# Cross-attention on one Trainium2 core: in each key tile TensorE does the side piece between the scores and the values

## The reference

```python
xq = ada_ln(x, cond, Wss_q, bss_q)            # x: (1, 4096, 512) f32
xkv = ada_ln(ctx, cond, Wss_kv, bss_kv)       # ctx: (1, 3202, 512) f32
q = (xq @ Wq + bq).reshape(B, Lq, 16, 32)
k, v = split((xkv @ Wkv + bkv).reshape(B, Lkv, 2, 16, 32))
scores = einsum('bqhd,bkhd->bhqk', q, k) / sqrt(32)
attn = softmax(scores, axis=-1)
out = einsum('bhqk,bkhd->bqhd', attn, v).reshape(B, Lq, 512)
return x + (out @ Wp + bp)
```

## Time and profile before

| | before |
|---|---|
| median of 3 runs | 2190.83 us |
| the profiled execution's own time | 2191.92 us |
| its span, first to last instruction | 2189.9 us |
| PE busy | 2162.7 us (99%) |
| DVE busy | 1895.0 us (87%) |
| ACT busy | 1820.4 us (83%) |
| granted TensorE clock, mean | 0.998 |

### The profile page before, as it was taken

How to read it: one execution, slowest core, us unless ns; L and a number is a source line. 1 busy time by engine, 2 the same in 40 slices (tenths; PEclk the granted TensorE clock), 3 DMA queues, 4 the chain that set the end, 5 groups by cost and what they waited for, 6 DMA issues and landing times.

```text
span 2189.9 us, 56660 instructions
## 1 busy us (share of the span) xinstructions
PE 2162.7 (99%) x25402; PEld 627.7 (29%) x25402; DVE 1895.0 (87%) x1098; ACT 1820.4 (83%) x1908; POOL 29.7 (1%) x29
## 2 busy tenths in 40 slices
PE   7999999999999999999999999999999999999998
PEld 3444322222222222222222222222222222222222
DVE  2321799989999899999999999989999999989998
ACT  1212899999999999999999899999999999999995
POOL 0000000000000000000000000000000000000000
PEclk9999999999999999999999999999999999999999
DMA  7322322223222422223222422223222322232211
GB/s 283 116 96 91 118 62 61 60 68 118 66 65 71 116 64 62 71 66 115 70 64 67 116 71 60 67 75 117 60 72 59 109 64 67 60 99 88 66 44 41
DMA packets 171445, 180.91 MB, mean 83 GB/s; under 512 B 14006, under 2 KB 117182, under 8 KB 171196
## 3 DMA queue, kind: packets, MB, share of 16 engines
q1 hardware_dynamic: 169612, 176.70, 27.0%
q10 hardware_dynamic: 1584, 0.53, 0.1%
HBM read 146.27 MB, written 30.92 MB: 81 GB/s over the span
## 4 chain that ended last, share of the span: by engine, by line
PE 97%; DMA 1%; DVE 1%; issue 0%; ACT 0%; SPq 0%; POOL 0%; DVEq 0%
PE bank L1024 39%; PE bank L1036 36%; PE bank L942 5%; PE bank L1112 4%; PE bank L1066 4%; PE bank L953 4%; PE bank L1048 1%; PE bank L1077 1%; PE bank L922 1%; DMA arena<-l_recip 1%; PE bank L1174 1%; PE bank L1088 1%; DMA arena<-in_ctx_dram 0%; DMA l_recip<-r_blk 0%; PE bank L1098 0%
## 5 line engine op out<-in xcount | busy, mean ns | idle before, releaser
L1282 ACT ACTIVATE arena<-bank,shift 128x1024 f32<-128x1024 f32 x1600 | 1692.2, 1113 | 162.2 <-PE bank L1024 154.5
L1567 DVE TENSOR_TENSOR arena<-arena 128x2048 f32<-128x2048 f32 x736 | 1669.7, 2289 | 110.4 <-ACT arena L1282 98.0
L1024 PE MATMUL bank<-qs,ks 32*64 32x512 f32 x12800 | 922.1, 613 | 1.1 <-ACT arena L1246 0.7
L1036 PE MATMUL bank<-arena,vg 128*32 128x512 f32 x6400 | 852.3, 605 | 1.3 <-ACT arena L1282 1.3
L1036 PEld LDWEIGHTS bank<-arena,vg 128*32 128x32 f32 x6400 | 125.9, 108 | 650.6 <-ACT arena L1282 649.0
L1024 PEld LDWEIGHTS bank<-qs,ks 32*64 32x64 f32 x12800 | 206.7, 129 | 346.8 <-ACT arena L1282 204.0
L1112 PE MATMUL bank<-wp,arena 128*32 128x168 f32 (+2 forms) x2464 | 153.6, 321 | 1.6 <-DVE arena L1496 1.6
L1066 PE MATMUL bank<-xt,wq 128*32 128x256 f32 x1792 | 137.7, 379 | 0.0
L1112 PEld LDWEIGHTS bank<-wp,arena 128*32 128x32 f32 x2464 | 80.0, 110 | 186.5 <-issue 170.0
L1433 DVE TENSOR_TENSOR arena<-bank,bv_b 128x512 f32<-128x512 f32 x25 | 17.3, 691 | 127.2 <-PE bank L953 127.1
L1246 ACT ACTIVATE arena<-bank,bk_c 128x512 f32<-128x512 f32 (+1 forms) x28 | 18.0, 642 | 130.8 <-PE bank L942 130.8
(11 more groups left out here) (90 smaller groups left out, 430.3 us busy)
## 6 DMA issues: line engine op xcount, KB each, us to landing
ks<-k_full SPq DMA_DIRECT2D x160, 320.0 KB, 3.1
vg<-v_full SPq DMA_DIRECT2D x160, 320.0 KB, 3.7
xin<-in_x_dram SPq DMA_DIRECT2D x9, 1024.0 KB, 9.9
q_full<-qs SPq DMA_DIRECT2D x32, 256.0 KB, 2.1
out_dram<-arena SPq DMA_DIRECT2D x32, 256.0 KB, 2.1
arena<-l_recip SPq DMA_DIRECT2D x28, 256.0 KB, 5.8
arena<-in_x_dram SPq DMA_DIRECT2D x7, 1024.0 KB, 10.2
arena<-in_ctx_dram SPq DMA_DIRECT2D x6, 1024.0 KB, 7.9
```

What stands on the lines that cost most here:

```text
L1024: mm = nc.tensor.matmul(bank[out, 2 * (i % RING) + h % 2, :], ks[rows_of(h), keys], qs[rows_of(h), g, :], start=True, stop=True)
L1036: mm = nc.tensor.matmul(bank[rows_of(h), o_bank(u), :], vg[:, t, rows_of(h)], pt[t % PR][:, h, :], start=(t == 0), stop=False, skip_group_ ...
L1282: nc.scalar.activation(pt[t % PR][:, 2 * pair:2 * pair + 2, :], bank[:, first:first + 2, :], ACT.Exp, scale=SCALE, bias=shift[:, g:g + 1]) ...
L1567: nc.vector.tensor_tensor(a[:, :, :], (pt[t - 1] if k <= 2 else a)[:, :, :], pt[t % PR][:, :, :], ALU.add).then_inc(p_added, 1)
```

## The change

In the loop over the key tiles the side piece moves from behind `weigh` to ahead of it, for all tiles but the first of a unit. The two halves of `weigh_tail` stay behind `weigh`, in the same tiles as before (15 and 24 for g = 0, 22 and 24 for g > 0); they leave `first_side` and `later_side` and stand in the loop. No instruction is added or taken away, and the other engines' programs are as before.

```diff
@@ first_side
-                        if t in (15, 24):
-                            weigh_tail(u, t // 24)
@@ later_side
-                        if t in (22, 24):
-                            weigh_tail(u, t // 24)
@@ the loop over the units and tiles, behind scores(u, t + 1)
-                            weigh(u, t)
+                            if t == 0:
+                                weigh(u, t)
                             if g == 0:
                                 first_side(u, b, t)
                             else:
                                 later_side(u, b, g, t)
+                            if t > 0:
+                                weigh(u, t)
+                            if t in ((15, 24) if g == 0 else (22, 24)):
+                                weigh_tail(u, t // 24)
```

## The result

| | before | after |
|---|---|---|
| median | 2190.15 us (4 runs, 2188.64 to 2191.17) | 2223.59 us (4 runs, 2223.08 to 2223.8) |
| span of the profiled execution | 2189.9 us | 2221.6 us |
| PE, DVE, ACT busy | 2162.7, 1895.0, 1820.4 us | 2169.2, 1895.8, 1821.2 us |

The ratio is 1.0152 (95% interval 1.0138 to 1.0166): 33.4 us slower. The forecast was 2234.3 us, 43.5 slower in the prediction's sum. The stage ahead of the attention, which the change leaves alone, took 227.95 us in the profiled execution before and 225.71 after (start of the first scores). From there to the start of the last full tile it is 1933.66 before and 1968.69 after: the change itself costs 35.0 us in the traces.

What follows compares the result with a forecast made beforehand. The prediction took PE's own sequence per tile as the bound. Stalls of 15.0, 12.3, 9.0, 1.6, 6.3 and 0.3 summed to 44.5 us, less 1 for ring waits, giving 2234.3 us, range 2225 to 2246 (wider 2210 to 2258).

Steps and rivals of the forecast that it cites:

- The side tiles are at PE's own pace: Tiles with a 256-column side piece: scores to next group 1.04, period 2.47 us in either order, so no tile gains.
- What it adds is a wait in front of the values: A job's first piece, now ahead of the values, waits for ScalarE's take of the job before, 157 times; the stall is lost whole.
- the signal: Time from the end of ScalarE's take to the waiting piece's start, taken as 0.11 us, with 0.06 and 0.15 as ends.
- The narrow pieces: Side pieces of 168 and 176 columns; behind a stall they meet the wait inside the scores less often, taken as -1 us.
- take of 176 or 168 columns: Stall ahead of denominators, output job 2 and queries at t = 14: 60 x 0.25 = 15.0 us.
- tiles 10 to 14 of g = 0, together: Each tile waits for a take; 0.47 + 0.43 give 0.9 a block, 7 x 0.9 = 6.3 us.
- The transposing tiles: 28 transposing pieces of form 128x128: new transitions taken as 0, bounded at 3 us either way.
- The division: Output piece waiting for DVE loses 0.88 us of cover: nothing in block 4, some 0.8 in block 7, partly given back; net 0.3.
- Rival A: Weight-load waits in `weigh` are real, early loading shortens scores to side; -52 us, 2139; chance 0.09.
- Rival B: Stalls overlap: 0.1 to 0.15 off each of the 157 stalls, result +20 to +28, 2211 to 2219 us; chance 0.09.
- Rival C: After each of 157 waits PE also pays a restart, 0.15 each, +24 us: 2258; chance 0.13.
- D: Rival of no change: takes are in time if ScalarE's reported ends are late by 0.3; 2191 us; chance 0.03.

Runs made afterwards that it cites:

- the run with the quarters: Kernel before (values first), second half of weigh_tail cut into two quarters of 128 columns, tiles 23 and 24, units with g > 0: 2186.64 us, ratio 0.9980.

## Why the prediction came out as it did

**The side tiles are at PE's own pace: right.** Scores to the next group is 1.04 to 1.05 whatever follows, 2.47 in either order, and moving the 438 pieces that don't wait changes nothing (ratio 1.0001). The rule of the Trainium skill ("TensorE: Matmul & The Clock Gate", Step-by-step) on weight loads pulled ahead doesn't shorten this place. The loads of the values do run ahead, 0.21 before their matmuls (975.49 and 975.70), but the pieces of 975.25, whose weights wait for nothing, still come 1.05 behind the scores. Its other half, that matmuls keep their order, agrees with the stalls.

**What it adds is a wait in front of the values: right,** in place, count and mechanism. The pieces that wait are the loss (1.0158 alone against 1.0152 for all), and taking the activation out of their way takes nine tenths of it away.

**The stall of each kind was mis-sized by one term, the signal.** I took 0.11 between the end of the take and the piece. The trace after has 0.05 three times out of three (972.72 to 972.77, 978.05 to 978.10, and 2033.08 to 2033.13 for a narrow take), and 0.05 or 0.06 in nearly all of the others. In tile 12 of g = 0 the take of the tail ends 0.16 before the piece, which starts 1.05 behind the scores: that piece doesn't wait, so 150 of the 157 do. The 0.15 of the earlier trace rows was the end of a DVE instruction and no row for ACT; the 0.06 of the earlier trace rows was. The sum stood at 43.5 and the traces show 35.0, 8.5 less. The signal stands in the sum 123 times by itself and twice in the chains of each of seven blocks, and 137 x 0.06 is 8.2 us of that. The division makes another 0.5 (below). The narrow pieces met the ring wait less often than I had taken: they gave back 3.0 us and not 1, but the narrow stalls in tiles 10 and 14 were 0.24 for the same reason and not 0.19, so little of that is left. By kind:

| piece waits for | predicted | traces |
|---|---|---|
| take of 176 or 168 columns | 0.25 | 0.19 (tile 4), 0.24 (tiles 10 and 14) |
| denominators | 0.44 | 0.38 |
| queries | 0.32 | 0.26 |
| output of 256 columns | 0.23 | 0.17 |
| tiles 10 to 14 of g = 0, together | 0.9 | 0.86 (0.61 in block 0) |

**The transposing tiles: right,** 16.74 us for tiles 10 to 15 against 15.88 in blocks 1 to 6. The forms' transitions, kept at 0, cost nothing that shows.

**The division: near in block 7, wrong in what gives it back and in block 4.** In block 7 tile 16 lasts 4.02 in place of 3.03, 0.99 for the 0.88 of cover (predicted 0.8). The piece in tile 11 gives nothing back there: that tile stays at 3.23, because the ring wait stands inside the scores, ahead of both orders. I had that in the first part of the prediction and didn't use it here. In block 4 I took the division to cost nothing on top of the other stalls. But PE waited for it before as well, so these stalls passed in part while it would have waited anyway: tile 16 fell from 4.02 to 2.97. Over the seven blocks tile 16 changed by -0.2 us, where I had +0.3. None of these differences is exact, since this tile moves from one execution to the next. With the values first it lasted 4.02, 3.51 and 2.54 us in block 4 and 3.03, 3.30 and 3.79 in block 7, in the traces of the kernel before, of the run that moves only the pieces that wait for nothing, and of the run with the quarters.

Rival A (faster) needed 0.96 from scores to side and got 1.05. Rival B (half, +20 to +28) assumed 0.10 to 0.15 off each stall; 0.06 is what the signal gave, so the result of +33.4 fell between its range and that of the forecast. Rival C (restart costs) has nothing: behind a stall side to values is 0.46 (972.77 to 973.23), without one 0.45 (975.25 to 975.70). Of D nothing was seen.

## What to carry to other kernels

When two pieces of an in-order engine are swapped, look at what each waits for: the first now pays its wait whole, and what stood ahead of it was its cover. A long total of waiting weight loads is no prize when the distance between the matmuls' starts is the same in tiles where the awaited result came early. And a release must be priced from a row of the same pair of engines.

## What was not expected of the hardware

From the end of an ACT activation to the start of a matmul that waited for it: 0.05 us; from the end of a DVE operation 0.15 (and 2000.92 to 2001.07 in the changed kernel, in the next fence). A take on ScalarE has two covers to use up, that of the piece and that of the ring; 0.16 us more of it cost 0.18 us with the piece first, and 0.11 to 0.18 with the values first.

```profile
1998.63 2.29 DVE L1497 TENSOR_TENSOR arena<-o_all,arena 128x2048 f32<-128x2048 f32 x1 [1.73 <-DMA arena<-l_recip]
...
2001.07 0.64 PE L1112 MATMUL bank<-wp,arena 128*32 128x256 f32 x8 [1.48 <-DVE arena L1497]
```
